# The first score product of a batch placed behind the AV products of the iteration before

## The chip, the cores and the metric

One Trainium2 chip, one core of it. The metric is the device time of one execution in microseconds. TensorE (PE), VectorE (DVE), ScalarE (ACT), GpSimd (POOL) and SyncE (SP) run their own instruction streams in order and meet at semaphores. All DMAs of this part of the kernel are issued by SP.

## The reference

Thirty-two batches of x (256 rows of 256) and a context of the same shape pass through four gated residual steps: a divergence attention with an MLP, a product with weights quantised to FP8, a 16-head cross attention, and an MLP with dequantised weights:

```python
query = _split_heads(q @ w_q.T + b_q)
key = _split_heads(k @ w_k.T + b_k)
value = _split_heads(v @ w_v.T + b_v)
scores = jnp.einsum('bhqd,bhkd->bhqk', query, key) / jnp.sqrt(jnp.asarray(D_K, query.dtype))
scores = jnp.where(mask == 0, jnp.asarray(-1000000000.0, scores.dtype), scores)
attn = jax.nn.softmax(scores, axis=-1)
out = jnp.einsum('bhqk,bhkd->bhqd', attn, value)
...
x = x + jnp.tanh(g_xattn[1]) * _L1_xattn_ref(_layernorm(x, axis=-1), ctx_1024, ctx_1024, mask_Bx1xSxS2_if1, ...)
```

The change is in the 16-head attention. Its mask is all ones in these inputs.

## The kernel before, in words

The kernel has two phases with a barrier between. `phase_a` does the first attention and its MLP for all batches; it isn't touched. `phase_b` does the other three steps as a software pipeline: each engine runs a loop over iterations, and in one iteration it works on up to eight batches, each one stage further on. `lagged` gives them the names n, f, q, m, a, o, h, w (lags 0 to 7): q projects queries, keys and values, m takes the maxima of the scores, a does exponentials and the AV products, o the output projection, h and w the last MLP. So batch q of one iteration is batch m of the next and batch a of the one after. Thirty-two batches take 39 iterations; 28 of them have all stages from q to h filled. `pipeline` writes out the first five pairs and the last ones and loops over the rest.

TensorE's order within an iteration is written out by hand (the calls at the end of its `iteration`). It starts with the transposes of the heads' outputs of o (`heads_transposed`, L1987, two groups of four), with `scores(0)` of m between them, and goes on with transposes, projections, `scores(1)` to `scores(7)` of m and `scores_transposed(0)` to `(7)` of a in turn, and ends with `values(2)`, `values(3)` (AV products of a, L1910), `hidden(2)`, `hidden(3)` (L1835, of h) and `values_in` (the V projection of q, L1835).

The scores need the queries and keys as stacks of high and low bfloat16 parts with 48 rows per head: Q4 and K4, two buffers each, by the batch's parity. VectorE and ScalarE make the parts (`qs`, `ks`), SP spills them to DRAM (`spill_queries` L1267, `spill_keys` L1262) and loads them as stacks with six DMAs of 64 KB each (`stack_queries` L1290, `stack_keys` L1279). The stacks of q have the buffers of batch q-2, which is a of the same iteration; so both wait for all eight `scores_transposed` of a:

```python
if (due := done(q, back=2, per=NP)) is not None:
    sp.wait_ge(sig["scoreT_mm"], due)
```

`scores(i)` (L1875) waits, for i = 0, for the landing of all twelve stack DMAs, and for VectorE's reduction of the pair before (`maxima`, L1653), since there is one tile of PSUM for scores; for i = 0 this is `maxima(7)` of the batch before. `maxima` puts the negated maxima of the rows into `nm`; SP transposes them (`transpose_maxima`, L1315), puts them as a row into Q4 (`row_of_maxima`, L1323), and `scores_transposed` (L1892) then gives scores less maximum for ScalarE's exponential (L1471).

SP's order per iteration: `load_context`, `transpose_rounded` (four transposing DMAs yT<-y, L1306), the spills and stacks of q, `transpose_maxima` of m, `load_mask` of q, `row_of_maxima` of m, `store`. The mask goes to `mask_in` (one buffer), and VectorE makes `mb` from it one iteration later (`mask_bias` of m, L1626, ahead of `maxima(7)`). TensorE has two copies of its pipeline, and a value loaded at the start chooses; without a masked position it takes the one that neither waits for `mb` nor multiplies by it.

The PSUM banks of TensorE's other products are used in turns (`TURNS`, `bank_free`): the transposes of xh (`normalised_transposed`, L1843) take bank 7 after ScalarE has copied V out of it (`values_copy`, L1520); the second head group takes bank 9 after `silu(3)`.

Of the kernel before, what the change touches and what calls it, by code (L numbers as in the profile page):

```python
# [6 lines left out]
ALU = mybir.AluOpType  # L7
# [36 lines left out]
def lagged(half, parity, lag, batches):  # L44

    if isinstance(half, int) and not 0 <= 2 * half + parity - lag < batches:
        return None
    return Batch(half + (parity - lag) // 2, (parity - lag) % 2)
# [34 lines left out]
def done(batch, back=0, per=1, part=None):  # L83


    count = (batch.number - back) * per + (per if part is None else part)
    return count if not isinstance(count, int) or count > 0 else None


def landed(batch, back=0, per=1):  # L90


    half = batch.half + (batch.parity - back) // 2
    count = 16 * per * (half + 1)
    return count if not isinstance(count, int) or count > 0 else None
# [1016 lines left out]
def phase_b(nc, a, NB, out_d, ctxT_d, mask_d, X, mu1, rsq, scale_qk, gate, ident, identb, minus_half, f1, f2, b1f, any_masked,  # L1112
# [9 lines left out]
    NP = NH // 2  # L1122
    HALF = P // 2
    MINUS = -2.0 ** 60
# [3 lines left out]
    with scope:  # L1128
        def sb(name, shape, dt):
            return scope.enter_context(nc.sbuf_tensor("b_" + name, shape, dt))  # L1130

        def two(name, shape, dt):
            return [sb(f"{name}_{i}", shape, dt) for i in range(2)]
# [23 lines left out]
        mask_in = sb("mask_in", [P, T, S], I32)  # L1157
        mb = two("mb", [P, T, S], BF16)
# [48 lines left out]
        sig = Signals(nc, "b_")  # L1207
# [29 lines left out]
        def _(sp):  # L1237
# [5 lines left out]
            def iteration(half, parity):  # L1243
                n, f, q, m, a, o, h, w = [lagged(half, parity, lag, NB) for lag in range(8)]
# [8 lines left out]
                def load_mask():  # L1253
                    at = bass.ds(q.number, 1)
                    if (due := done(q, back=1)) is not None:
                        sp.wait_ge(sig["mb"], due)
                    sp.dma_start(mask_in[:, :, :], mask_d[at].rearrange("o p t s -> p (o t) s")).then_inc(
                        sig[f"mask{q.parity}"], 16)

                def spill_keys():  # L1260
                    sp.wait_ge(sig["klo"], done(q))
                    sp.dma_start(k_dram[q.parity].rearrange("s (c p) n -> p (s c) n", p=P),  # L1262
                                 ks[:, :, :, :].rearrange("p s c n -> p (s c) n")).then_inc(sig[f"kspill{q.parity}"], 16)

                def spill_queries():
                    sp.wait_ge(sig["qlo"], done(q))
                    sp.dma_start(q_dram[q.parity].rearrange("s (c p) n -> p (s c) n", p=P),  # L1267
                                 qs[:, :, :, :].rearrange("p s c n -> p (s c) n")).then_inc(sig[f"qspill{q.parity}"], 16)
# [14 lines left out]
                def stack_queries():  # L1283
                    sp.wait_ge(sig[f"qspill{q.parity}"], landed(q))
                    if (due := done(q, back=2, per=NP)) is not None:
                        sp.wait_ge(sig["scoreT_mm"], due)
                    for odd in range(2):
                        for r, (part, _) in enumerate(TERMS):
                            rows = slice(odd * HALF + r * DK, odd * HALF + (r + 1) * DK)
                            sp.dma_start(Q4[q.parity][rows, :, :],  # L1290
                                         q_dram[q.parity][part].rearrange("(h e d) n -> e d h n", e=2, d=DK)[odd]).then_inc(
                                sig[f"qstack{q.parity}"], 16)
# [6 lines left out]
                def transpose_rounded():  # L1299
                    sp.wait_ge(sig["y"], done(f))  # L1300
                    if (due := done(f, back=1)) is not None:
                        sp.wait_ge(sig["ffn_mm"], due)
                    sp.sem_inc(sig["y_ready"], 1)
                    for c in range(C):
                        for t in range(T):
                            sp.dma_start(yT[:, c, t * P:(t + 1) * P], y[:, t, c * P:(c + 1) * P],  # L1306
                                         transpose=True).then_inc(sig[f"yT{f.parity}"], 16)
# [18 lines left out]
                if f:  # L1326
                    load_context()
                    transpose_rounded()
                if q:
                    spill_queries()  # L1330
                    spill_keys()
                    stack_queries()
                    stack_keys()
                if m:
                    transpose_maxima()
                if q:
                    load_mask()
                if m:
                    row_of_maxima()
                if w:  # L1340
# [245 lines left out]
        def _(dve):  # L1586
# [28 lines left out]
            def iteration(half, parity):  # L1615
                n, f, q, m, a, o, h, w = [lagged(half, parity, lag, NB) for lag in range(8)]
# [3 lines left out]
                    nc.vector.tensor_tensor(xT[:, 1], whole_bank(BANK["xT"]), xT[:, 0], ALU.subtract).then_inc(sig["xlo"], 1)  # L1620

                def mask_bias():
                    dve.wait_ge(sig[f"mask{m.parity}"], landed(m))
                    if (due := done(m, back=2, per=NP)) is not None:
                        dve.wait_ge(sig["scoreT_mm"], due)
                    nc.vector.tensor_scalar(mb[m.parity][:, :, :], mask_in[:, :, :], 0.0, MINUS, ALU.is_equal,  # L1626
                                            ALU.mult).then_inc(sig["mb"], 1)

                def mlp_normalised():
# [47 lines left out]
                def statistics_2():  # L1677
                    dve.wait_ge(sig["x2"], done(f))
                    statistics(st2, mv2, "2", f)
# [122 lines left out]
                    result()  # L1802
                if f:
                    statistics_2()
                if m:
                    mask_bias()
                    maxima(7)
                if f:
                    attention_normalised()
# [11 lines left out]
                if at_iteration(half, parity, 5):  # L1821
# [3 lines left out]
                                            f2[:, 0].rearrange("p h d -> p (h d)"), ALU.subtract).then_inc(sig["f2lo"], 1)  # L1825

            pipeline(dve, iteration, NB, LAGS)

        @block.tensor
        def _(pe):  # L1830
# [15 lines left out]
            def tile(t):  # L1846
                return slice(t * P, (t + 1) * P)

            def iteration(half, parity, mask):
                n, f, q, m, a, o, h, w = [lagged(half, parity, lag, NB) for lag in range(8)]  # L1850

                def free(name):
                    bank_free(pe, half, parity, name)
# [7 lines left out]
                                                    second["b_col"][:, c:c + 1], start=c == 0, stop=c == C - 1)  # L1861
                    last.then_inc(sig["b1_mm"], 1)

                def scores(i):
                    if i == 0:
                        pe.wait_ge(sig[f"kstack{m.parity}"], landed(m, per=6))
                        pe.wait_ge(sig[f"qstack{m.parity}"], landed(m, per=6))
                        if mask:
                            pe.wait_ge(sig["mb"], done(m))
                    if (due := done(m, per=NP, part=i)) is not None:  # L1870
                        pe.wait_ge(sig["nm"], due)
                    for t in range(T):
                        for odd in range(2):
                            rows = slice(odd * HALF, odd * HALF + TOP)
                            last = nc.tensor.matmul(score_ps[:, odd, t], Q4[m.parity][rows, i, tile(t)],  # L1875
                                                    K4[m.parity][rows, i, :], start=True, stop=not mask)
                        for odd in range(2 if mask else 0):
                            last = nc.tensor.matmul(score_ps[:, odd, t], identb[:, :], mb[m.parity][:, t, :],
                                                    start=False, stop=True)
                    last.then_inc(sig["score_mm"], 1)  # L1880
# [19 lines left out]
                def values(g):  # L1900
                    if g == 0:
                        pe.wait_ge(sig["V"], done(a))
                    name = ("AV01", "AV23")[g // 2]
                    if g % 2 == 0:
                        free(name)
                    pe.wait_ge(sig["E"], done(a, per=NP, part=2 * g + 2))
                    for k in range(T):
                        for j in range(HG):
                            i = HG * g + j
                            last = nc.tensor.matmul(bank[BANK[name]][ONE * j:ONE * (j + 1), g % 2, :], V[a.parity][:, k, i, :],  # L1910
                                                    E[:, i % RING, k, :], start=k == 0, stop=k == T - 1,
                                                    tile_position=(0, ONE * j))
                    last.then_inc(sig["av_mm"], 1)
# [85 lines left out]

                if o:  # L2000
                    heads_transposed(0)
                if m:
                    scores(0)
                if o:
                    heads_transposed(1)
                if q:
                    normalised_transposed()
# [56 lines left out]
                if a:  # L2064
                    values(2)
                    values(3)
                if h:
                    hidden(2)
                    hidden(3)
# [55 lines left out]
```

## Time and profile before

| | us |
|---|---|
| median of 3 runs | 1614.0 (1612.15 to 1616.75) |
| span of the profiled execution | 1614.4 (its only time on record) |
| busy TensorE, matmuls | 1486.5 (92%) |
| busy VectorE | 1316.4 (82%) |
| busy ScalarE | 1135.2 (70%) |
| busy GpSimd | 1034.7 (64%) |
| mean granted TensorE clock | 0.969 of full speed |

Busy times are sums over the instructions of an engine. Matmuls are pipelined and their ends modelled, so neighbouring rows of TensorE overlap a little. The first matmul of the second phase starts at about 622 us, the first `scores(0)` at 650.85, the last at 1522.82. Times in rows are from the start of the span.

### The profile page before, as it was taken

The page shows a single profiled execution, that of the slowest core. Times are in us where ns is not written, and L with a number is a line of the kernel's source. Part 1 is how long each engine was busy: PE and PEld are TensorE (multiplying, and loading weights), DVE is VectorE, ACT ScalarE, POOL GpSimd, SP SyncE. Part 2 cuts the span into 40 slices and gives each one's busy share as a digit, 9 for nine tenths or more (in the row PEclk, how much of TensorE's full clock was granted, in tenths as well). Part 3 has the DMA queues.
Part 4 walks back from the last instruction along what each step waited for, and adds up shares of the span by engine and source line. Part 5 has one row for each costly group of instructions (what it writes and reads, how often), then busy time and mean ns, then how long its engine had stood idle before and what let it go on. Part 6 is the DMA issues. An engine that isn't in the chain of part 4 may idle for free.

```text
span 1614.4 us, 42641 instructions
## 1 busy us (share of the span) xinstructions
PE 1486.5 (92%) x14155; PEld 1144.6 (71%) x14155; DVE 1316.4 (82%) x3187; ACT 1135.2 (70%) x2057; POOL 1034.7 (64%) x1392
## 2 busy tenths in 40 slices
PE   4999999999999972668999999999999999999997
PEld 2788888888888861435667676777777776777666
DVE  4698888888888875778988889898988889898742
ACT  7798888888888742355666666666666666676664
POOL 4588888888888744224556565665656566565445
PEclk9999999999999995588999999999999999999999
DMA  7322222322222002332223232232223232232200
GB/s 228 96 80 66 91 72 65 96 66 69 93 65 71 2 1 92 80 119 73 80 80 87 73 85 80 85 87 81 83 78 92 72 91 74 86 85 84 64 16 22
DMA packets 197690, 125.45 MB, mean 78 GB/s; under 512 B 44400, under 2 KB 196848, under 8 KB 197360
## 3 DMA queue, kind: packets, MB, share of 16 engines
q1 hardware_dynamic: 197616, 124.48, 26.2%
q8 instruction: 44, 0.72, 0.2%
q14 instruction: 30, 0.25, 0.1%
HBM read 92.69 MB, written 25.17 MB: 73 GB/s over the span
## 4 chain that ended last, share of the span: by engine, by line
PE 48%; SPq 4%; DVE 3%; issue 2%; DMA 2%; POOL 2%; ACT 1%; POOLq 0%
PE b_bank L1835 28%; PE b_bank L1910 7%; PE b_scoreT L1892 4%; PE b_score L1875 4%; PE b_bank L1843 2%; PE b_bank L1987 1%; SPq L1306 1%; DMA b_nmT<-b_nm 1%; DMA b_yT<-b_y 1%; SPq L1290 1%; DVE b_nm L1653 1%; SPq L1279 1%; PE b_bank L1925 1%; ACT b_E L1471 1%; SPq L1315 0%
## 5 line engine op out<-in xcount | busy, mean ns | idle before, releaser
L1471 ACT ACTIVATE b_E<-b_scoreT 128x1024 f32<-128x1024 f32 x256 | 262.2, 1024 | 152.5 <-PE b_scoreT L1892 151.3
L1653 DVE TENSOR_REDUCE b_nm<-b_score 128x4 bf16<-128x1024 f32 x256 | 313.3, 1224 | 54.6 <-PE b_score L1875 48.4
L31 ACT ACT_TABLE_LOAD x157 | 201.4, 1283 | 18.6 <-PEq L1059 15.2
L1835 PE MATMUL b_bank<-f,b_YT 128*128 128x256 bf16 x1536 | 190.3, 274 | 4.7 <-POOL b_YT L1404 4.6
L890 PE MATMUL bank<-hT,W1T 128*128 128x256 bf16 x1536 | 183.3, 273 | 2.4 <-DVE hT L706 1.7
L1835 PE MATMUL b_bank<-b_hT,f 128*128 128x256 bf16 x1536 | 183.4, 273 | 0.8 <-DVE X L1749 0.8
L890 PE MATMUL bank<-W2T,G 128*128 128x256 bf16 x1024 | 171.0, 272 | 6.7 <-DVE GT L780 6.2
L1835 PEld LDWEIGHTS b_bank<-f,b_YT 128*128 128x128 bf16 x1536 | 143.5, 98 | 39.7 <-issue 19.5
L1835 PEld LDWEIGHTS b_bank<-b_hT,f 128*128 128x128 bf16 x1536 | 147.7, 98 | 30.3 <-issue 12.6
L890 PEld LDWEIGHTS bank<-hT,W1T 128*128 128x128 bf16 x1536 | 148.0, 98 | 27.7 <-ACT G L549 4.0
L1388 POOL TENSOR_TENSOR b_v<-b_v,b_e 128x512 f32<-128x512 f32 x32 | 40.6, 1269 | 195.0 <-DVE b_e L1734 195.0
L1404 POOL TENSOR_TENSOR b_YT<-b_Y,b_YT 128x512 bf16<-128x512 f32 x128 | 148.9, 1163 | 10.7
L1401 POOL TENSOR_SCALAR b_YT<-b_Y 128x512 bf16<-128x512 f32 x128 | 82.2, 642 | 104.2 <-ACT b_Y L1531 97.5
L1531 ACT ACTIVATE b_Y<-b_bank,b1f 128x256 f32<-128x256 f32 x256 | 104.2, 473 | 51.4 <-PE b_bank L1835 51.0
L890 PE MATMUL bank<-W2T,GT 128*128 128x256 bf16 x512 | 139.5, 273 | 0.0
L1910 PE MATMUL b_bank<-b_E,b_V 128*32 128x256 f32 x2048 | 134.0, 392 | 0.0
L1875 PE MATMUL b_score<-b_K,b_Q 48*128 48x256 bf16 x1024 | 102.7, 280 | 24.1 <-DVE b_nm L1653 13.1
L549 ACT ACTIVATE G<-bank,b1c 128x256 f32<-128x256 f32 x256 | 103.7, 467 | 29.4 <-PE bank L890 29.4
L890 PEld LDWEIGHTS bank<-W2T,G 128*128 128x128 bf16 x1024 | 98.3, 98 | 23.2 <-issue 12.6
L1892 PE MATMUL b_scoreT<-b_Q,b_K 49*128 49x256 bf16 x1024 | 100.7, 275 | 8.6 <-ACT b_E L1471 6.2
L1742 DVE TENSOR_SCALAR b_xh<-X,b_mv,b_rs 128x256 f32 (+1 forms) x64 | 61.9, 1006 | 43.7 <-POOL b_rs L1382 43.7
L1910 PEld LDWEIGHTS b_bank<-b_E,b_V 128*32 128x32 f32 x2048 | 57.7, 111 | 49.8 <-issue 23.4
(222 smaller groups left out, 3524.8 us busy)
## 6 DMA issues: line engine op xcount, KB each, us to landing
b_Q<-q_dram SPq DMA_DIRECT2D x192, 64.0 KB, 2.6
b_K<-k_dram SPq DMA_DIRECT2D x192, 64.0 KB, 2.8
xin<-in_x SPq DMA_DIRECT2D x32, 256.0 KB, 3.2
ctxn<-in_ctx SPq DMA_DIRECT2D x32, 256.0 KB, 2.8
mask_in<-in_mask SPq DMA_DIRECT2D x32, 256.0 KB, 3.0
X<-in_x SPq DMA_DIRECT2D x32, 256.0 KB, 4.0
ctxt<-in_ctxT SPq DMA_DIRECT2D x32, 256.0 KB, 4.2
b_ctxt<-in_ctxT SPq DMA_DIRECT2D x32, 256.0 KB, 2.8
```

The source lines that it names most:

```text
L31: act.add_instruction(mybir.InstLoadActFuncSet(name=nc.get_next_instruction_name(), act_func_set_id=which, ins=[], outs=[]))
L549: last = nc.scalar.activation(G[:, 2 * j + i], mlp_ps[j % 2][:, i], ACT.Gelu, bias=b1c[:, 2 * j + i:2 * j + i + 1])
L890: last = nc.tensor.matmul(out_tile, lhs(i, k), rhs(j, k), start=k == 0 and (i, j) == TERMS[0], stop=k == chunks[-1] and (i, j) == TERMS[-1])
L1401: nc.gpsimd.tensor_scalar(YT[:, 0, 2 * j:2 * j + 2], Y[:, 2 * j:2 * j + 2], 1.0, 0.0, ALU.mult, ALU.add).then_inc(sig["Yhi"], 1)
L1404: nc.gpsimd.tensor_tensor(YT[:, 1, 2 * j:2 * j + 2], Y[:, 2 * j:2 * j + 2], YT[:, 0, 2 * j:2 * j + 2], ALU.subtract).then_inc(sig["Ylo"], 1)
L1471: nc.scalar.activation(E[:, pair:pair + 2], scoreT_ps[:, :, :, :], ACT.Exp).then_inc(sig["E"], 1)
L1531: last = nc.scalar.activation(Y[:, 2 * j + i], bank[BANK[f"H{j}"]][:, i], ACT.Silu, bias=b1f[:, 2 * j + i:2 * j + i + 1])
L1653: nc.vector.tensor_reduce(pair, score_ps[:, :, :, :], AX.X, ALU.max, negate=True).then_inc(sig["nm"], 1)
L1835: last = nc.tensor.matmul(out_tile, lhs(i, k), rhs(j, k), start=start and k == chunks[0] and (i, j) == TERMS[0], stop=stop and k == chunks ...
L1875: last = nc.tensor.matmul(score_ps[:, odd, t], Q4[m.parity][rows, i, tile(t)], K4[m.parity][rows, i, :], start=True, stop=not mask)
L1892: last = nc.tensor.matmul(scoreT_ps[:, odd, k], K4[a.parity][rows, i, tile(k)], Q4[a.parity][rows, i, :], start=True, stop=not mask)
L1910: last = nc.tensor.matmul(bank[BANK[name]][ONE * j:ONE * (j + 1), g % 2, :], V[a.parity][:, k, i, :], E[:, i % RING, k, :], start=k == 0, ...
```

## The change

SP issues `load_mask` of q ahead of the spills instead of behind `transpose_maxima`. VectorE's `mask_bias` works on q instead of m, so one iteration earlier, at the same place of its list. TensorE's `scores(0)` of a batch leaves the start of the iteration in which the batch is m and stands behind `values(3)` of the iteration in which it is q, ahead of `hidden(2)`; its waits go with it. The two groups of `heads_transposed` then follow each other.

```diff
@@ SP
                     load_context()
                     transpose_rounded()
                 if q:
+                    load_mask()
                     spill_queries()
                     spill_keys()
                     stack_queries()
                     stack_keys()
                 if m:
                     transpose_maxima()
-                if q:
-                    load_mask()
                 if m:
                     row_of_maxima()
@@ VectorE
                 def mask_bias():
-                    dve.wait_ge(sig[f"mask{m.parity}"], landed(m))
-                    if (due := done(m, back=2, per=NP)) is not None:
+                    dve.wait_ge(sig[f"mask{q.parity}"], landed(q))
+                    if (due := done(q, back=2, per=NP)) is not None:
                         dve.wait_ge(sig["scoreT_mm"], due)
-                    nc.vector.tensor_scalar(mb[m.parity][:, :, :], mask_in[:, :, :], 0.0, MINUS, ALU.is_equal,
+                    nc.vector.tensor_scalar(mb[q.parity][:, :, :], mask_in[:, :, :], 0.0, MINUS, ALU.is_equal,
                                             ALU.mult).then_inc(sig["mb"], 1)
...
-                if m:
+                if q:
                     mask_bias()
+                if m:
                     maxima(7)
@@ TensorE
-                def scores(i):
+                def scores(i, m=m):
...
                 if o:
                     heads_transposed(0)
-                if m:
-                    scores(0)
-                if o:
                     heads_transposed(1)
...
                 if a:
                     values(2)
                     values(3)
+                if q:
+                    scores(0, q)
                 if h:
                     hidden(2)
                     hidden(3)
```

## Rows read from the trace of the kernel before

**Rows 1.** Busy time by engine, two stretches; start:end, length, busy (instructions) each, granted clock

```profile
1105.08:1132.88 27.80, 27.80 (x298) 20.10 (x297) 24.45 (x51) 18.85 (x29) 17.05 (x22) 1.00 0.28 83
...
909.36:1467.22 557.86, 557.33 (x5922) 401.40 (x5921) 494.94 (x1002) 377.48 (x580) 340.93 (x440) 1.00 0.29 83
```

**Rows 2.** Waits of TensorE, whole kernel: us, times, longest

```profile
PE b_bank L1925 <- DMA b_yT<-b_y: 17.5, 5, 12.6
...
PE b_score L1875 <- DMA b_K<-k_dram: 11.0, 3, 9.2
...
PE b_bank L1843 <- DVE b_on L1703: 7.2, 2, 5.3
```

**Rows 3.** Waits of SP's queue, 900 to 1450 us: us, times, longest

```profile
SPq L1290 <- PE b_scoreT L1892: 60.4, 20, 3.1
```

**Rows 4.** Order of time, all engines: start, us, engine line op out<-in [idle before]

```profile
1123.49 0.11 PEld L1892 LDWEIGHTS b_scoreT<-b_Q,b_K 49*128 49x128 bf16 x4 [0.21 <-issue]
...
1123.92 2.69 SPq L1290 DMA_DIRECT2D b_Q<-q_dram  x6
...
1126.72 2.73 SPq L1279 DMA_DIRECT2D b_K<-k_dram  x6
...
1127.59 1.23 DVE L1653 TENSOR_REDUCE b_nm<-b_score 128x4 bf16<-128x1024 f32 x1
...
1128.95 2.79 PE L1835 MATMUL b_bank<-b_hT,f 128*128 128x256 bf16 x24
...
1133.43 0.39 PE L1875 MATMUL b_score<-b_K,b_Q 48*128 48x256 bf16 x4
```

**Rows 5.** K4's issues and the wait for them in the fill; landing of all K4 DMAs

```profile
697.97 2.74 SPq L1279 DMA_DIRECT2D b_K<-k_dram  x6
...
703.07 0.39 PE L1875 MATMUL b_score<-b_K,b_Q 48*128 48x256 bf16 x4 [0.83 <-DMA b_K<-k_dram]
...
DMA to landing us min/median/max: 2.3/2.8/3.7
```

**Rows 6.** K4's issues and the product behind values(3), first and last; a long Q4 issue

```profile
788.43 2.75 SPq L1279 DMA_DIRECT2D b_K<-k_dram  x6
...
790.61 2.79 PE L1835 MATMUL b_bank<-b_hT,f 128*128 128x256 bf16 x24
...
813.49 3.87 SPq L1290 DMA_DIRECT2D b_Q<-q_dram  x6
...
1516.19 2.73 SPq L1279 DMA_DIRECT2D b_K<-k_dram  x6
...
1518.34 2.79 PE L1835 MATMUL b_bank<-b_hT,f 128*128 128x256 bf16 x24
```

**Rows 7.** The fill, batch 1: K4's issues, and where TensorE stands

```profile
668.63 2.79 SPq L1279 DMA_DIRECT2D b_K<-k_dram  x6
...
668.92 2.74 PE L1835 MATMUL b_bank<-wqkvo,b_cT 128*128 128x256 bf16 x12
```

**Rows 8.** Order of time at the head transposes, and the copy of V

```profile
1105.10 0.60 PE L1987 MATMUL b_bank<-ident,b_oS 128*128 128x128 f32 x4
...
1105.39 0.66 ACT L1520 ACTIVATE b_V<-b_bank 128x256 f32<-128x256 f32 x2 [0.56 <-PE b_bank L1835]
...
1105.96 0.66 PE L1987 MATMUL b_bank<-ident,b_oS 128*128 128x128 f32 x4
...
1106.45 0.60 PE L1843 MATMUL b_bank<-ident,b_xh 128*128 128x128 f32 x4
```

**Rows 9.** Two gaps of TensorE and the stretches behind them (columns as rows 1)

```profile
716.12 0.60 PE L1925 MATMUL b_bank<-wf,b_yT 128*128 128x256 bf16 x4 [2.89 <-DMA b_yT<-b_y]
...
593.00:597.00 4.00, 4.00 (x39) 3.59 (x37) 3.66 (x11) 3.19 (x3) 1.64 (x3) 1.00 0.01 4
...
716.00:720.00 4.00, 3.88 (x33) 1.60 (x34) 2.44 (x5) 1.07 (x2) 1.16 (x1) 0.61 0.00 0
...
592.53 0.38 PE L890 MATMUL bank<-W2T,G 128*128 128x256 bf16 x2 [2.38 <-DVE GT L780]
```

More of the change, by code:

```diff
@@ L1804, in iteration @@
                     statistics_2()
+                if q:
+                    mask_bias()
                 if m:
-                    mask_bias()
                     maxima(7)
```

## The prediction

> **What bounds the kernel now.** I read the table of stretches first, to see which engine is full in one repeating iteration of the second phase, then the waits of TensorE and of SP's queue, then one iteration in order of time around the place the change touches. In the iteration from 1105.08 us TensorE is busy 27.80 of 27.80 us, and over twenty iterations (909.36 to 1467.22) 557.33 of 557.86, that is 27.9 each; VectorE has about 3 us of air per iteration, ScalarE 9 [rows 1]. TensorE takes its instructions in a hand-written order, so a microsecond of waiting put into that order is a microsecond of kernel, unless a wait elsewhere gives it back. It has almost none to give: over the whole kernel the K4 stack's landing costs it 11.0 us in 3 waits, all while the second phase fills [rows 2].
>
> The order of time shows what the move meets [rows 4]. The last `scores_transposed(7)` starts at 1123.49. SP has been waiting for it (60.4 us in 20 waits in the stretch asked, 3 each) [rows 3], because Q4 and K4 of batch q have the parity of batch a, which that product is the last to read. At 1123.92 SP issues the six DMAs of Q4 (2.69 us of queue time), at 1126.72 the six of K4 (2.73 us, to 1129.45). TensorE meanwhile ends `values(2)`, `values(3)` and starts `hidden(2)` at 1128.95. The next iteration's `scores(0)` starts only at 1133.43, behind `hidden(2)`, `hidden(3)`, `values_in` and four transposes: 4.5 us that today hide the landing.
>
> **When K4 is there.** In the fill TensorE really waited for it: K4's six DMAs start at 697.97 and take 2.74, to 700.71; `scores(0)` starts at 703.07, so 2.36 us after the last issue ended [rows 5]. The bounds for one DMA are 2.3 and 3.7 us from issue to landing, median 2.8 (same group); the last is issued about 0.46 before the end, so 1.8 to 3.2 us behind it. I take 2.36, since it is the same wait itself; the bounds would move each stall by -0.5 and +0.9 us.
>
> **The change part by part.**
>
> 1. `scores(0, q)` behind `values(3)`. TensorE could start it at 1128.95; K4 is there at 1129.45 + 2.36 = 1131.81. The wait is 2.86 us, and `hidden(2)`, `hidden(3)`, `values_in` and all that follows queue behind it. The trigger, `scores_transposed(7)`, shifts with TensorE, so the wait can't wear off: it is new in each iteration. I took the same difference (end of K4's issues + 2.36 - start of `hidden(2)`) for the 28 batches 4 to 31: it is 2.93 for batch 5, 2.94 for batch 31, and 2.85 to 2.94 in these and 21 more, 2.87 on average [rows 6]; in the other five SP needed longer for Q4's or K4's issues (3.87 us for Q4's in the one shown), 5.6 us more together. 28 x 2.87 + 5.6 = 86 us.
> 2. The same in the fill. Batch 1: K4's issues end at 671.42, landing at 673.8, TensorE is ready at 668.92: 4.9 us. Batch 0 waits 9.2 us anyway [rows 2], but its `values_in`, 2.74 us at the low clock, now comes behind the wait instead of ahead [rows 7]; some of it is caught up, 2 us. Batches 2 and 3 lose the cover of `values_in` and `heads_transposed(0)`, 1.9 us each. Sum 11 us.
> 3. Given back: waits on engines that get 2.9 us of air per iteration. TensorE waits 7.2 us in two places for VectorE's `b_on` while the second set of weights is prepared, the longer 5.3: one stall of 2.9 can go from that and all of the other 1.9, 4.8 us. Of the 17.5 us for the DMAs of yT, 12.6 are one wait at the phase's start [rows 2]; I count 2 us of the rest. 7 us in all; bounds 0 and 12.
> 4. The two groups of head transposes. Today `scores(0)` stands between them: 0.86 us from group to group; two neighbouring groups of transposes are 0.49 apart [rows 8], so 0.37 is saved, and `scores(0)` costs at most its own 0.39 [rows 4] in its new place. But `normalised_transposed` comes earlier, at about 1106.08, and its bank is free only when ScalarE has copied V (1105.39 + 0.66 = 1106.05, and a signal) [rows 8]: 0.1 to 0.2 us. Together +3 us over 28 iterations; bounds -10 (no new wait, `scores` free) and +6.
> 5. SP. `load_mask` goes ahead of the spills: one issue of about half a microsecond between the yT transposes and the Q spill. SP waits 3 us for `scores_transposed(7)` later in the same list [rows 3], and the mask buffer was freed an iteration earlier, so this costs nothing; without that cover it would be 0.5 per iteration. Row of maxima and store don't gain either: they wait for the landing of the maxima, as now.
> 6. VectorE. `mask_bias` is done for q instead of m, the same instruction in the same place; TensorE takes the branch without mask, so nobody waits for it. The wait of `scores(0, q)` for `maxima(7)` of batch m, which ends at 1127.59 + 1.23 = 1128.82 [rows 4], is over before K4 is there: nothing. Without the K4 wait it would cost about 0.1.
> 7. The clock. The stalls are a new kind of gap. After a gap of 2.89 us at 716.12 the next 4 us show a granted clock of 0.61, so partly 1.2 GHz instead of 2.4; the loss is 0.39 x 4 plus a rest, 1.7 us. After 2.38 us at 592.53, with dense products on both sides, it stayed at 1.00 [rows 9]. Our gap is as long as the first and has dense neighbours like the second. Bounds: none of some 30 stalls (0 us) and all (51 us). I take one in four, 13 us, nearer to the row that is like it in kind.
>
> The Trainium skill, page "TensorE: Matmul & The Clock Gate", section "Loop structure matters more than you think", speaks against this change: a loop in which TensorE waits for a DMA ahead of its matmuls runs them at the low clock. By that rule the clock would fall after each stall and the sum would be 38 us higher than mine; that time is rival C, and the rows bear it out in one case of the two.
>
> On the landing, the page "DMA: Bandwidth & Descriptors" of the Trainium skill, section "Anatomy of one DMA — SWDGE (gpsimd) path", gives about 2.0 us fixed plus bytes over 436 GB/s (fitted to DMAs issued from GpSimd), 2.15 us for 64 KB by my estimate. The trace has a median of 2.8 for the same transfer, so it decides. With 2.15 the landing would be 0.65 us earlier and the sum some 20 us lower.
>
> **Sum.** The profiled execution spans 1614.4 us; the runs shown have a median of 1614.0, so nothing of note lies around it. 1614.4 + 86 + 11 - 7 + 3 + 13 = 1720.
>
> **The rivals.**
>
> *A. Forecast: the K4 wait binds in each iteration, clock mostly held.* With the clock never falling 1707, with half of the stalls 1733. Chance 0.65.
>
> *B. Faster: K4 isn't late.* Place: the end of `values(3)`. It decides from the point where K4 has landed by 1128.95, 2.86 us earlier than worked out, for example if the issue of the stacks isn't tied to `scores_transposed(7)` as I read it. Then only the saving of step 4 is left, at most 0.37 x 28 = 10 us, and waits given back: 1604. Against it: SP's wait for `scores_transposed(7)` is on record [rows 3], and the Q4 issue follows that product's start by 0.43 us. Chance 0.03.
>
> *C. The clock falls after each stall.* 51 instead of 13: 1758; from half of them on, 1733. For it: equal length to the 2.89 gap. Against: the dense neighbours. Chance 0.2.
>
> *D. The wait is shorter.* With the landing at its lower bound each stall is 0.5 us shorter, 15 us less, and with a clock that never falls 13 less again: 1692. For it: the lower bound is on record. Against it: the one wait for K4 that I can read to the end came out at 2.36, and no transfer is taken away from beside this one. Chance 0.1.
>
> *E. The change does nothing:* the landing is hidden all the same, and gain and cost of the reordering cancel, 1614. Chance 0.02.
>
> **How the numbers follow.** A change of 0.3% is about the least that a measurement of this kernel can tell from none. A, C and D are all slower by far: 0.95; B is 0.03 faster; E 0.02 same. The range takes A, most of C and nearly D's end: 1693 to 1753.
>
> **What the profile after would show.** Right: a wait of `scores(0)` (the first of the score products) for the DMA of K4 of about 2.9 us in each iteration, some 95 us in total against 11.0; iterations of 30.7 to 30.8 us in the steady stretch where the clock holds; VectorE's reduction no later than now in the next iteration; SP's queue still waiting for `scores_transposed(7)`. Step 4: the two head groups 0.5 us apart, a small wait of the xh transposes for ScalarE's V. Step 7: the granted clock in the steady stretch just under 1.00 (at 0.25 of 30 stalls), 0.9 if C. Wrong: if the wait is for VectorE's maxima, or if iterations stay at 27.9 us.

## The result, and the profile after

The changed kernel takes 1720.5 us (median of 4 runs, 1713.2 to 1726.1) against 1615.4 (1612.2 to 1622.2) for the kernel before: a ratio of 1.0636, 95% interval 1.0591 to 1.0681. That is 105 us slower. The profiled execution spans 1724.2 us. Its chain of work by engine and by line:

```profile
PE 43%; SPq 9%; DMA 5%; issue 2%; DVE 2%; POOL 1%; ACT 1%; POOLq 0%
PE b_bank L1835 27%; DMA b_K<-k_dram 5%; SPq L1290 5%; PE b_scoreT L1892 4%; SPq L1279 4%; PE b_bank L1910 4%; PE b_score L1875 4%; PE b_bank L1843 3%; PE b_bank L1987 1%; PE b_bank L1925 1%; DMA b_yT<-b_y 0%; ACT b_E L1470 0%; SPq L1306 0%; DVE b_nm L1652 0%; PE b_scoreT L1860 0%
```

TensorE is 87% busy, before it was 92%; every other engine does the same work as before in a longer time. SP's queue has gone from 4% to 9% of the chain and DMA from 2% to 5%, and the lines are named: the issues of Q4 (L1290) and K4 (L1279) and K4's landing. The waits of TensorE over the whole kernel (us, times, longest) answer to [rows 2]:

```profile
PE b_score L1875 <- DMA b_K<-k_dram: 105.9, 32, 11.7
PE b_bank L1925 <- DMA b_yT<-b_y: 15.6, 3, 12.6
...
PE b_bank L1843 <- DVE b_on L1702: 6.2, 2, 5.9
```

One row has moved by much: the wait for K4 is 105.9 us in 32 waits, one for each batch, where it was 11.0 in 3. The difference, 94.9 us, is most of the 110 us between the two profiled spans. One iteration in order of time (start, us, engine line op, idle before), to be laid beside [rows 4] and [rows 8]:

```profile
1124.76 0.39 PE L1892 MATMUL b_scoreT<-b_Q,b_K 49*128 49x256 bf16 x4
...
1125.19 2.69 SPq L1290 DMA_DIRECT2D b_Q<-q_dram  x6
...
1127.99 2.74 SPq L1279 DMA_DIRECT2D b_K<-k_dram  x6
...
1128.77 1.22 DVE L1652 TENSOR_REDUCE b_nm<-b_score 128x4 bf16<-128x1024 f32 x1
...
1133.01 0.39 PE L1875 MATMUL b_score<-b_K,b_Q 48*128 48x256 bf16 x4 [2.72 <-DMA b_K<-k_dram]
...
1133.33 2.79 PE L1835 MATMUL b_bank<-b_hT,f 128*128 128x256 bf16 x24
...
1137.27 1.04 PE L1987 MATMUL b_bank<-ident,b_oS 128*128 128x128 f32 x8
...
1137.57 0.66 ACT L1519 ACTIVATE b_V<-b_bank 128x256 f32<-128x256 f32 x2 [0.57 <-PE b_bank L1835]
...
1138.37 0.65 PE L1843 MATMUL b_bank<-ident,b_xh 128*128 128x128 f32 x4
```

Up to the AV products nothing has changed. K4's issues end at 1130.73, `scores(0)` starts 2.28 us later and stood idle for 2.72 us, and `hidden(2)` starts 8.57 us behind `scores_transposed(7)` instead of 5.46. VectorE's last reduction ended at 1129.99, three microseconds before it was wanted. From the head transposes of the iteration before, at 1106.74, to these at 1137.27 it is 30.53 us, and 30.67 to the next at 1167.94; in the kernel before the iteration of [rows 4] took 27.79 and the next one 27.93.

The second, smaller part is the clock. After the stall at 1255.54 the hidden products, 2.79 us for 24 matmuls at full speed, take almost double; first the products, then the granted clock in that stretch (columns as in [rows 1]):

```profile
1255.54 0.61 PE L1875 MATMUL b_score<-b_K,b_Q 48*128 48x256 bf16 x4 [2.82 <-DMA b_K<-k_dram]
1256.09 5.30 PE L1835 MATMUL b_bank<-b_hT,f 128*128 128x256 bf16 x24
```

```profile
1256.09:1261.00 4.91, 4.91 (x26) 3.48 (x25) 1.38 (x5) 0.84 (x2) 0.00 (x0) 0.50 0.17 55
```

Nine of the 28 full iterations have such slow hidden products, wholly or in part at 1.2 GHz where they were at 2.4. Their 24 matmuls, and the V projection where it was still slow, took 1.2 to 2.7 us more each, 16.6 us together. In the kernel before there is none in those places. 94.9 + 16.6 is 112 against 110 between the two profiled spans.

### The profile page after: what moved, and what is told of

It is laid out like the page before. It is cut to its first block, busy times and chain, and to the rows that moved or that the text cites. A ratio compares the mean times of both kernels' runs of the same rounds, so it can differ in the third digit from the quotient of the medians.

```text
span 1724.2 us, 42619 instructions
## 1 busy us (share of the span) xinstructions
PE 1505.4 (87%) x14155; PEld 1157.3 (67%) x14155; DVE 1306.8 (76%) x3187; ACT 1132.4 (66%) x2057; POOL 1026.4 (60%) x1392
## 4 chain that ended last, share of the span: by engine, by line
PE 43%; SPq 9%; DMA 5%; issue 2%; DVE 2%; POOL 1%; ACT 1%; POOLq 0%
PE b_bank L1835 27%; DMA b_K<-k_dram 5%; SPq L1290 5%; PE b_scoreT L1892 4%; SPq L1279 4%; PE b_bank L1910 4%; PE b_score L1875 4%; PE b_bank L1843 3%; PE b_bank L1987 1%; PE b_bank L1925 1%; DMA b_yT<-b_y 0%; ACT b_E L1470 0%; SPq L1306 0%; DVE b_nm L1652 0%; PE b_scoreT L1860 0%
## 5 line engine op out<-in xcount | busy, mean ns | idle before, releaser
L1875 PE MATMUL b_score<-b_K,b_Q 48*128 48x256 bf16 x1024 | 104.1, 283 | 118.3 <-DMA b_K<-k_dram 105.9
L1835 PE MATMUL b_bank<-b_hT,f 128*128 128x256 bf16 x1536 | 199.4, 288 | 0.8 <-DVE X L1748 0.8
L1835 PEld LDWEIGHTS b_bank<-b_hT,f 128*128 128x128 bf16 x1536 | 155.5, 103 | 33.4 <-issue 8.1
L1875 PEld LDWEIGHTS b_score<-b_K,b_Q 48*128 48x128 bf16 x1024 | 34.6, 95 | 184.6 <-issue 117.6
L1372 POOL TENSOR_SCALAR b_cT<-b_ctxt 128x512 bf16<-128x512 f32 x32 | 19.8, 617 | 165.3 <-PE b_bank L1835 165.2
L890 PEld LDWEIGHTS bank<-W2T,G 128*128 128x128 bf16 x1024 | 98.3, 98 | 23.1 <-issue 12.5
L1697 DVE RECIPROCAL b_rsum<-b_bank 128x16 f32<-128x16 f32 x64 | 16.2, 253 | 124.9 <-PE b_bank L1987 124.9
```

The lines of the kernel that those rows point to most:

```text
L890: last = nc.tensor.matmul(out_tile, lhs(i, k), rhs(j, k), start=k == 0 and (i, j) == TERMS[0], stop=k == chunks[-1] and (i, j) == TERMS[-1])
L1835: last = nc.tensor.matmul(out_tile, lhs(i, k), rhs(j, k), start=start and k == chunks[0] and (i, j) == TERMS[0], stop=stop and k == chunks ...
```

## The experiments

Each kernel is compared with runs of the kernel before that were made with it; these had medians between 1616.9 and 1618.1.

**Is it the mask's part?** SP's and VectorE's edits alone, TensorE's order as before:

```diff
 if q:
+    load_mask()
     spill_queries()
...
-if m:
+if q:
     mask_bias()
```

> Only the mask's part of the change: load_mask ahead of the spills, mask_bias one iteration earlier; TensorE's order as before. Theory (the whole loss is the wait of scores(0) for K4): same as before, 1612 to 1618 us, wait for K4 11 us as before. Rival (SP's new order delays the spills and so the stacks): half a microsecond per iteration or more, 1630 us or above, with SP's stack issues later against scores_transposed(7).

1617.6 us, ratio 0.9995 (0.9977 to 1.0014). Steady iterations are 27.79 and 27.85 us long, the wait for K4 12.8 us in 3 waits. The mask's part costs nothing that can be told from none, within 3 us.

**Is it joining the head transposes?** The kernel before, with only this:

```diff
 heads_transposed(0)
-scores(0)
 heads_transposed(1)
+scores(0)
```

> The kernel before with the two head groups joined and scores(0) of m behind them, in the same iteration as before. Theory: K4 is there, so nothing is waited for; the scores cost the same in either place: 1610 to 1618 us. Rival (joining the head transposes costs, because the next transposes then wait for ScalarE's copy of V): up to 0.3 us in 28 iterations, 1623 us.

1617.9 us, ratio 1.0002 (0.9985 to 1.0019). Within 3 us it costs nothing and brings nothing.

**Is it running the scores an iteration ahead, or the place?** Two kernels with the whole change, but `scores(0, q)` at other places of the same iteration's end. The first:

```diff
 values(3)
-scores(0, q)
 hidden(2)
 hidden(3)
+scores(0, q)
 values_in()
```

> The change, but with scores(0, q) behind hidden(2) and hidden(3) instead of ahead of them. Theory: 2.64 of the 2.86 us are covered; left are some tenths per iteration, the fill's 11 us and the wait for the copy of V (0.3 x 28): 1625 to 1638 us, the wait for K4 some 0.1 to 1.5 us per iteration. Rival (the loss comes from running the first scores an iteration ahead at all, through VectorE's maxima or the order of SP): stays above 1690 us.

The second:

```diff
 values(3)
-scores(0, q)
 hidden(2)
 hidden(3)
 values_in()
+scores(0, q)
```

> The change, but with scores(0, q) as the last product of the iteration, behind values_in. Theory: all of the landing is covered as before, and no wait for the copy of V: 1610 to 1619 us, wait for K4 about 11 us in the fill only. Rival as in the run before: above 1690 us.

Behind `hidden(3)`: 1634.7 us, ratio 1.0093 (1.0064 to 1.0123), K4 waited for 32.4 us in 21 waits, most of that time in the fill: in the stretch from 1000 to 1500 us it is 3.2. Behind `values_in`: 1620.7 us, ratio 1.0019 (1.0001 to 1.0038), with steady iterations of 27.87 us, within 0.01 of the mean of 27.79 and 27.93 before. That is 1.7 us above the upper end of what was expected; the wait for K4 is 14.3 us in 5 waits, where 11 were expected. So the same product, an iteration ahead, costs between 0 and 105 us by how much work stands between `scores_transposed(7)` and it. What is left in the second kernel is 3 us, hardly more than the measurement can tell; the longer wait for K4 in the fill would account for it, but nothing here shows that.

**Is `scores_transposed(7)` the trigger?** The changed kernel with it 12 matmuls earlier:

```diff
 second_product(1, 0)
+scores_transposed(7)
 hidden(0)
-scores_transposed(7)
 scores(6)
```

> The changed kernel with scores_transposed(7) moved ahead of hidden(0), 12 matmuls or 1.31 us. Theory: SP is released 1.31 us earlier and the wait is 1.31 us shorter, 1.5 us per iteration; 28 x 1.31 = 37 us less and, with gaps of 1.5 us, no falls of the clock (13 us less): about 1670 us (1660 to 1685). Rival (the wait is set by something else than this product, such as the K spill): no change, 1715 to 1725 us.

1677.7 us, ratio 1.0374 (1.0349 to 1.0400). Steady iterations are 29.2 to 29.5 us instead of 30.6: about 1.3 less, which is the distance moved. The clock fell in 4 iterations, where none was expected to; each had a gap of 2.0 us or more. After the usual gaps of 1.1 to 1.5 us, and after one of 1.65, it held.

**What does the clock cost?** The changed kernel with matmuls of no use in the gap:

```diff
 def scores(i, m=m):
     if i == 0:
+        if a and h:
+            pe.wait_ge(sig["nm"], done(m, per=NP, part=0))
+            for k in range(20):
+                nc.tensor.matmul(score_ps[:, 0, 0], f1[:, 0, 0, 0:P], hT[:, 0, 0], start=True, stop=True)
         pe.wait_ge(sig[f"kstack{m.parity}"], landed(m, per=6))
```

> The changed kernel with 20 matmuls (128x128 by 256, about 2.2 us) that do nothing of use put into the wait ahead of scores(0, q), in the iterations that have hidden products. Theory: K4 arrives when it did, so the wait shrinks by what the filler takes, and iterations with the clock at full speed last as long as now (30.6 us); the clock no longer falls after the wait, which is worth 9 falls of 1.2 to 2.6 us: 1700 to 1710 us, mean clock up to 0.965. Rival (the falls cost nothing, they are hidden by later waits): 1715 to 1725 us. Other rival (the filler ends after K4): above 1725 us.

1708.5 us, ratio 1.0568 (1.0544 to 1.0592). One slow iteration instead of nine, steady iterations as long as in the changed kernel at full clock (30.3 to 30.8). Doing useless work in the gap makes the kernel 12 us faster, in line with the 16.6 read from the trace.

**What does one more issue ahead of K4 cost?**

```diff
-load_mask()
 spill_queries()
 spill_keys()
 stack_queries()
+load_mask()
 stack_keys()
```

> The changed kernel with load_mask between the issues of Q4 and of K4, so K4 is issued one DMA issue later (0.4 to 0.6 us). Theory: each of 32 waits is that much longer: 14 to 19 us more than the change, 1733 to 1742 us, wait for K4 about 120 us. Rival (slack in SP's queue absorbs it): 1715 to 1725 us.

1799.7 us, ratio 1.1145 (1.1123 to 1.1167): 79 us more than the change, where 14 to 19 were expected. One iteration shows what came on top:

```profile
1150.72 0.40 SPq L1257 DMA_DIRECT2D b_mask_in<-in_mask  x1
...
1151.23 2.77 SPq L1279 DMA_DIRECT2D b_K<-k_dram  x6
...
1154.18 0.43 DVE L1625 TENSOR_SCALAR b_mb<-b_mask_in 128x512 bf16<-128x512 int32 x1 [2.90 <-DMA b_mask_in<-in_mask]
1154.52 1.22 DVE L1652 TENSOR_REDUCE b_nm<-b_score 128x4 bf16<-128x1024 f32 x1
...
1156.39 0.61 PE L1875 MATMUL b_score<-b_K,b_Q 48*128 48x256 bf16 x4 [3.37 <-DMA b_K<-k_dram]
```

The gap is 3.37 instead of 2.72 us (mostly 3.0 to 4.1 over the iterations, up to 5.5), as it should be with one issue more and a little later landing. VectorE now waits 2.9 us for the mask too, and its `maxima(7)` ends only at 1155.74, 0.65 before `scores(0)`: hardly hidden any more. And the hidden products are slow (those behind this gap take 5.30 us instead of 2.79): in 28 iterations, not 9. Two candidates, so one more kernel, the same with useless matmuls in the gap (into the bank that `hidden(2)` overwrites, so they don't wait for the maxima):

```diff
     if i == 0:
+        if a and h:
+            free("H2")
+            for k in range(26):
+                nc.tensor.matmul(bank[BANK["H2"]][:, 0], f1[:, 0, 0, 0:P], hT[:, 0, 0], start=True, stop=True)
```

> The kernel with load_mask between the stacks' issues, which came out at 1800 us, plus 26 matmuls that do nothing of use (128x128 by 256, some 2.8 us) in the wait, into the bank that hidden(2) overwrites. Theory: K4 comes 0.5 us later, as expected then, and the other 60 us were the clock, which fell in 28 of 30 waits: with TensorE kept at work 1720 to 1738 us, at most 3 falls, mean clock 0.95 or more. Rival (the mask load delays something else, such as VectorE's mask_bias, maxima(7) and SP's transposes of the maxima behind it): above 1770 us.

1733.1 us, ratio 1.0710 (1.0665 to 1.0755), one slow iteration. So 67 of the 79 us went with the gap being filled: they were the clock. The rest, against 1708.5 for the filled changed kernel, is 25 us, 0.7 to 0.9 per iteration, for the extra issue (0.5) and the later landing (K4's median is 3.0 instead of 2.7 us). VectorE's lateness adds little: its reduction came after K4 in 5 of the 28 waits without the filling and in 2 with it, by 0.5 us at most.

**Issues or transfers?** Q4's six DMAs issued by ScalarE, beside SP's six of K4:

```diff
@@ SP
-stack_queries()
 stack_keys()
@@ ScalarE (the same function, with act.wait_ge and act.dma_start)
 exponential(7)
+if q:
+    stack_queries()
 load_functions(nc, act, SILU)
```

> The changed kernel with the six DMAs of Q4 issued by ScalarE behind its last exponential, beside SP's six of K4. Theory (12 issues in a row on one queue behind scores_transposed(7) make K4 late): K4 lands 2.8 us earlier, the wait of scores(0) falls from 2.8 to 0.1 to 0.5 us per iteration; ScalarE is held 2.7 us ahead of silu(0), which may come back as waits for its copies, so 1625 to 1655 us. Rival (the transfers themselves or DRAM's answer are what takes long): 12 transfers together are no faster, above 1700 us.

1796.8 us, ratio 1.1120 (1.1083 to 1.1158). The theory's forecast failed by over 140 us, and for the reason the rival gives:

```profile
1140.66 2.69 SPq L1279 DMA_DIRECT2D b_K<-k_dram  x6
...
1140.76 2.73 ACTq L1540 DMA_DIRECT2D b_Q<-q_dram  x6
...
1149.73 0.61 PE L1887 MATMUL b_score<-b_K,b_Q 48*128 48x256 bf16 x4 [3.98 <-DMA b_Q<-q_dram]
```

All twelve are issued by 1143.5, yet `scores(0)` can start only at 1149.73, 9.07 us behind the first issue; on one queue it was 7.82. The two stretches from the first issue to `scores(0)`, of the changed kernel and of this one (the last three columns are granted clock, DMA share, GB/s):

```profile
1125.19:1133.01 7.82, 5.10 (x65) 3.33 (x62) 5.66 (x12) 4.47 (x7) 4.25 (x7) 1.00 0.37 105
```

```profile
1140.66:1149.73 9.07, 5.10 (x64) 3.31 (x61) 5.22 (x12) 4.36 (x7) 3.67 (x7) 0.91 0.84 94
```

The DMA engines count as busy 0.84 of the time instead of 0.37 and move fewer bytes per second: the two queues' transfers stand in each other's way. The median time to landing goes from 2.6 and 2.7 us to 5.0 and 4.6. The gap of 3.98 us brought 28 slow iterations again. With the gap filled by 34 useless matmuls (the edit is that of the kernel with the mask between and the gap filled, with 34 for 26):

> The kernel with Q4 issued by ScalarE, which came out at 1797 us, plus 34 matmuls that do nothing of use in the wait. Theory (landing 1.2 us later than with one queue, the rest of the loss the clock): 1740 to 1760 us, at most 3 falls of the clock. Rival (ScalarE held up by its issues costs the rest): above 1775 us.

1748.2 us, ratio 1.0804 (1.0754 to 1.0853), no slow iteration, mostly 32.0 to 32.4 us each. Against the filled changed kernel that is 40 us more, about 1.5 per iteration. In the stretch from 1000 to 1300 us `scores(0)` starts 9.3 to 9.5 us behind the first issue, against 7.6 to 8.0 in the filled changed kernel: the later landing is the whole of it, and nothing is left for ScalarE's time for the issues. So on two queues the transfers set the pace. Whether they do on one was still open, and two kernels took it apart. The first halves the bytes and keeps the issues (shown for K4, the same is done to Q4):

```diff
+heads = NP if at_batch(q, 0) or at_batch(q, 1) else NP // 2
...
-sp.dma_start(K4[q.parity][rows, :, :],
-             k_dram[q.parity][part].rearrange("(h e d) n -> e d h n", e=2, d=DK)[odd])
+sp.dma_start(K4[q.parity][rows, 0:heads, :],
+             k_dram[q.parity][part].rearrange("(h e d) n -> e d h n", e=2, d=DK)[odd][:, 0:heads])
```

> The changed kernel with each of the twelve stack DMAs loading only the first four of eight head rows from the third batch on, 32 KB instead of 64; the other heads keep the first two batches' data, so their scores are left out of the computation. Twelve issues as before. Theory (the issues set the pace on one queue): the wait for K4 stays within 0.3 us of 2.8, 1710 to 1724 us. Rival (the transfers set the pace, as ScalarE's queue beside SP's suggests, where K4 was no earlier): the wait falls below 1.8 us, 1675 to 1700 us.

The second keeps the bytes of each and issues two fewer:

```diff
-for r, (_, part) in enumerate(TERMS):
+for r, (_, part) in enumerate(TERMS[:2]):
...
-pe.wait_ge(sig[f"kstack{m.parity}"], landed(m, per=6))
+pe.wait_ge(sig[f"kstack{m.parity}"], landed(m, per=4))
```

> The changed kernel with four DMAs for K4 instead of six: the third group of rows isn't loaded and keeps its ones, so the product of the queries' low part with the keys is replaced by their sum. The last transfer keeps its 64 KB. Theory (12 issues of 0.45 us in a row set when the last one starts, and its own landing, which half the bytes shortened by 0.9 us, is added once): the wait falls by two issues, 0.9 us, from 2.7 to 1.8 us per iteration, 1690 to 1710 us with the clock as in the kernels before. Rival (all bytes together set the landing: one twelfth per DMA of what half of them gave, 0.3 us for two): the wait falls by 0.3 us, 1710 to 1720 us.

Half the bytes: 1704.9 us, ratio 1.0536 (1.0493 to 1.0579), between the two forecasts. Iterations at full clock are 29.7 us long, 0.9 less. The issues take what they took (2.67 and 2.70 us); what shrank is K4's time to landing. First the changed kernel's, then this one's:

```profile
DMA to landing us min/median/max: 2.3/2.7/3.4
```

```profile
DMA to landing us min/median/max: 1.7/1.8/3.5
```

Two fewer issues: 1697.8 us, ratio 1.0486 (1.0450 to 1.0522). The wait falls to 1.85 us, by 0.9, as for two issues of 0.45:

```profile
1142.17 0.40 PE L1875 MATMUL b_score<-b_K,b_Q 48*128 48x256 bf16 x4 [1.85 <-DMA b_K<-k_dram]
```

So on one queue the path is what the prediction took it for: SP's wait and start 0.43, twelve issues 5.5, and one landing 2.3, which depends on that transfer's bytes; together 8.2 us behind `scores_transposed(7)`, of which TensorE has work for 5.5. The clock spoils the totals of both kernels: it fell in 15 and in 11 iterations, more often than in the changed kernel, though the gaps are shorter.

## Why the prediction was right

The forecast was 1720 us, the median is 1720.5, and the mechanism is the one named, shown by moving the product, moving the trigger, taking issues away, adding one, and cutting the bytes.

- **Steps 1 and 2, the wait.** 2.86 us were worked out, 2.72 of idle measured in the iteration shown, with K4 2.28 instead of 2.36 us behind the last issue. The 28 waits of batches 4 to 31 sum to 82.8 us (forecast 86), the first four to 23.1, 12 more than before (forecast 11).
- **Step 3, given back.** 7 us were counted. The waits for `b_on` and for yT fell by 1.0 and 1.9 us, and the small waits for the row of maxima (2.1 us in 5 waits before) are gone: 5 us. The longer wait for `b_on` was to shrink by one stall; it went from 5.3 to 5.9. That part of the step failed: the stall doesn't give VectorE that time where it is late. And the 1.9 us of yT aren't shown to come from the stalls: in the first two experiments, whose times equal those of the kernel before, the same wait is 20.4 and 18.2 us.
- **Step 4.** From the first head transposes to those of xh it is 1.10 us against 1.35 [rows 8], and `scores(0)` adds 0.32: some 0.1 us per iteration more, 2 us (forecast 3). The wait for V's copy shows as one once, 0.7 us in the fill; elsewhere the xh transposes start 0.14 us behind the copy's end (1137.57 + 0.66), after a pause of 0.3 us under "issue".
- **Steps 5 and 6.** The mask's part of both is shown at nothing by the first experiment; that VectorE's maxima cost nothing is shown by their end at 1129.99, 3.0 us ahead of `scores(0)`. The price named for step 5 without its cover, 0.5 us, came out at 0.8 with the clock held, K4's later landing included.
- **Step 7, the clock.** One stall in four was taken, 13 us; it was nine of 28 and 16.6 us. This is the term that was least founded. The rival in which the clock falls after each stall became true with a gap some 0.7 us longer, where filling it gave 67 us. Its rule, of the Trainium skill's page "TensorE: Matmul & The Clock Gate" (section "Loop structure matters more than you think"), speaks of a long DMA wait between every matmul; taken for one gap per iteration, as the prediction took it, it holds in the two kernels with gaps of mostly 3.4 us and more. With 1.6 to 3 us it holds in part of the iterations, and with 1.1 to 1.5 in none.
- The landing by the page "DMA: Bandwidth & Descriptors" of the Trainium skill (section "Anatomy of one DMA — SWDGE (gpsimd) path"), an estimate of 2.15 us for 64 KB, would have made the kernel 20 us faster than forecast; K4's median is 2.7 and the trace decided rightly.

That the median was hit to half a microsecond is luck: the terms were off by -3, +1, +2, -1 and +4 us, which makes 1723 for the profiled execution of 1724.2, and the runs of this kernel spread over 13 us.

## What to carry to other kernels

Before a consumer is moved ahead, follow its operand back to what triggers the load: here a reuse of a buffer (`scores_transposed` of two batches before), then a row of issues on one queue, then one landing, 8.2 us that hung on a product 5.5 us ahead; the gap showed no wait in the profile, because 4.5 us of other work covered it. If such a product has to be moved, move it behind as much work as the path is long, or move the trigger: each microsecond of distance was worth one microsecond per iteration, until nothing is left to gain, since TensorE is full. And a stall on TensorE has a second price in its clock that isn't in proportion to the gap.

## What the runs showed that was not expected

How often the clock falls doesn't follow the length of the gap alone. Counted are iterations in which the hidden products behind it ran slow, in the one profiled execution of each kernel:

| kernel | wait for the stacks, us | slow iterations |
|---|---|---|
| behind `hidden(3)` (the V projection, which follows the gap here, ran no slower either) | 0 to 0.5 (four of 0.8 to 1.8) | 0 |
| trigger earlier | mostly 1.1 to 1.5 (four of 2.0 to 2.9) | 4 (those four) |
| two issues fewer | mostly 1.6 to 2.0 | 11 |
| half the bytes | mostly 1.9 | 15 |
| the change | 2.6 to 4.2, mostly 2.7 | 9 |
| mask between | 3.0 to 5.5, mostly 3.4 | 28 |
| two queues | 3.9 to 4.9, mostly 4.0 to 4.4 | 28 |
| the three with the gap filled | 2.7 to 4.0 with the filling | 1, 1, 0 |

Within the changed kernel its three gaps above 3.5 us (4.16, 3.92, 3.70) were each followed by slow products, but 3.13 and 3.19 were not and 2.71 was; seven of the nine slow ones lie before 1010 us. In the kernel before, a gap of 2.4 us left the clock at full speed [rows 9], while in its fill twelve matmuls at 707.56 took 2.69 instead of 1.47 us behind gaps of only 1.28 and 0.86 us, with TensorE busy for 1.86 of the 4.00 us from 704. How often it fell in the other three executions of the changed kernel isn't known: their mean granted clock was 0.951 to 0.956, in the profiled one 0.946. Why a gap of 1.9 us should be worse than one of 2.7 stays open, and neither kernel with gaps of 1.9 was run with its gap filled; the runs show that filling the longer gaps ends it.

A second queue made the same twelve transfers slower: 9.07 instead of 7.82 us to the last landing, at twice the DMA engines' busy share. Which resource they share wasn't tried.
